# Second attention with global keys laid out on the diagonal, global values made in two parts, and the layernorm's scaling on ScalarE

## The reference

```python
Q, K, V = x @ Wq.T + bq, x @ Wk.T + bk, x @ Wv.T + bv   # 16 heads of 8
local = softmax(Q K^T / sqrt(8), over the keys at most 32 places away) @ V
Kg, Vg = K[:, global_indices], V[:, global_indices]     # 25 keys, the same for all
glob = softmax(Q Kg^T / sqrt(8)) @ Vg                   # a softmax of its own
out = (0.7 * local + 0.3 * glob) @ Wo.T + bo
```

## Time and profile before

| | us |
|---|---|
| median of 3 runs | 1109.08 (1107.51 to 1109.56) |
| profiled execution | 1103.31 |
| its span | 1101.6 |
| TensorE busy | 953.2 (87%) |
| VectorE busy | 781.5 (71%) |
| ScalarE busy | 577.6 (52%) |
| GpSimd busy | 678.9 (62%) |

### The profile page before, as it was taken

The page is one execution under the profiler, slowest core; times in us unless marked ns, Lnnn a source line. Parts: engine busy times, 40 slices in busy tenths (PEclk is TensorE's granted clock), DMA queues, the critical chain, the costliest instruction groups (busy, mean ns, idle before and its releaser), DMA issues.

```text
span 1101.6 us, 27734 instructions
## 1 busy us (share of the span) xinstructions
PE 953.2 (87%) x7536; PEld 699.0 (63%) x7536; DVE 781.5 (71%) x3615; ACT 577.6 (52%) x1250; POOL 678.9 (62%) x1491
## 2 busy tenths in 40 slices
PE   3999999999959995799999999999999319999940
PEld 1777777777735552677777777777776218777830
DVE  3788888888825776457786877777775327888846
ACT  2566676666621332255555555555545007777734
POOL 3566666666631322266769888887879523777765
PEclk9899999999978998599999999999989559999975
DMA  6121111211042441111112121212211166777717
GB/s 184 27 52 32 45 45 31 48 27 45 23 132 91 161 164 80 32 47 34 47 29 59 39 59 48 68 44 60 53 32 38 44 173 234 238 234 250 254 58 212
DMA packets 71375, 98.34 MB, mean 89 GB/s; under 512 B 13688, under 2 KB 43256, under 8 KB 71104
## 3 DMA queue, kind: packets, MB, share of 16 engines
q1 hardware_dynamic: 61040, 83.31, 25.9%
q0 software_dynamic: 4992, 10.30, 2.8%
q10 hardware_dynamic: 5232, 3.42, 1.2%
HBM read 49.48 MB, written 24.77 MB: 67 GB/s over the span
## 4 chain that ended last, share of the span: by engine, by line
PE 73%; DVE 10%; issue 5%; DMA 3%; POOL 3%; ACT 2%; SPq 2%; DVEq 0%; ACTq 0%; POOLq 0%
PE bank L342 6%; PE bank L172 5%; PE bank L253 5%; PE bank L351 4%; PE bank L372 4%; PE bank L1491 4%; PE bank L1492 4%; PE bank L1257 4%; PE bank L1493 4%; PE bank L406 4%; PE bank L168 3%; PE bank L413 3%; PE bank L346 3%; PE bank L381 3%; PE bank L398 2%
## 5 line engine op out<-in xcount | busy, mean ns | idle before, releaser
L528 ACT ACTIVATE p<-bank 128x480 f32<-128x480 f32 (+1 forms) x448 | 240.5, 540 | 247.8 <-PE bank L372 88.0
L663 DVE CUSTOM_DVE_ANT_0 bank<-bank,band 128x160 f32<-128x160 f32 x512 | 156.9, 347 | 82.0 <-PE bank L342 79.5
L663 DVE CUSTOM_DVE_ANT_0 bank<-bank,causal 128x128 f32<-128x128 f32 (+1 forms) x512 | 169.4, 386 | 56.1 <-PE bank L346 40.3
L893 POOL TENSOR_SCALAR_AFFINE_SELECT p<-p 128x380 f32<-128x380 f32 (+1 forms) x256 | 146.5, 602 | 57.2 <-ACT p L528 56.2
L1669 POOL DMA_INDIRECT y_rows<-p,rows x92 | 105.9, 1151 | 67.5 <-DVE p L1622 46.2
L663 DVE DVE_READ_ACCUMULATOR2_ANT nm<- 128x1 f32 x1024 | 143.6, 140 | 0.1
L874 POOL TENSOR_SCALAR_AFFINE_SELECT p<-p 128x256 f32<-128x256 f32 (+1 forms) x192 | 91.0, 486 | 68.3 <-ACT p L528 64.6
L342 PE MATMUL bank<-ks,qs 128*128 128x186 f32 x512 | 118.6, 316 | 3.5 <-issue 2.3
L342 PEld LDWEIGHTS bank<-ks,qs 128*128 128x128 f32 x512 | 81.5, 198 | 38.2 <-issue 23.3
L372 PE MATMUL bank<-qs,ks 128*128 128x160 f32 x512 | 102.2, 303 | 0.0
L1562 ACT ACTIVATE p<-bank,wb 128x512 f32<-128x512 f32 x92 | 63.6, 691 | 39.5 <-PE bank L1493 37.6
(11 more groups left out here) (207 smaller groups left out, 2330.0 us busy)
## 6 DMA issues: line engine op xcount, KB each, us to landing
qs<-parts SPq DMA_DIRECT2D x46, 512.0 KB, 5.2
qs<-qf SPq DMA_DIRECT2D x128, 128.0 KB, 2.4
rows<-xr SPq DMA_DIRECT2D x23, 260.0 KB, 3.7
parts<-ks SPq DMA_DIRECT2D x8, 512.0 KB, 2.8
xs<-x_b SPq DMA_DIRECT2D x16, 256.0 KB, 4.0
p<-in_w SPq DMA_DIRECT2D x12, 256.0 KB, 3.4
xin<-in_x SPq DMA_DIRECT2D x16, 128.0 KB, 2.2
parts<-qf SPq DMA_DIRECT2D x4, 512.0 KB, 2.7
```

The source lines that it names most:

```text
L528: act.activation(pb[:, :, :].rearrange("p u c -> p (u c)")[:, lo:lo + cols], bank[:, 0:cols], ACT.Exp, scale=SCALE).then_inc(L.exp_done, 1)
L663: return dve.tensor_tensor_reduce(at, at, mask, -1.0, -BIG, ALU.add, ALU.min, nm[:, item:item + 1])
L893: pool.affine_select(out=at, in_=at, compare_op=ALU.is_ge, fill=0.0, base=base, pattern=[[0, 4], [sign, hi - lo]], channel_multiplier=-sig ...
```

## The change

- **Global keys.** Unit 3 of pass 2 exists only for j = 2 and j = 3, for the sequence before. Each handles two t with one 128-column stationary part (`kg`, 25 keys of each of the four j on a block diagonal) and the unspread queries `qf`, 256 columns, in fp32r. `lay_out_kg` (VectorE, at (1, 2)) fills `kg` from the keys in `ks` and a mask. The rows of maxima are therefore sent twice, into the spread queries and into `qf`, which becomes a ring of three.
- **Global values.** `global_values(0)` at (3, 1) and `global_values(1)` at (0, 1) of the next iteration: four matmuls each, with the exponentials (`pg`) stationary and 64 columns of `vgb` moving. They give the sums already turned, in `T.og`; the copy of `og` and `round_og` are gone, and `normalise` reads `T.og`.
- **Banks.** `og` leaves the bank order; `rp` and `rt`, products of the routing, move to the end of (1, 1). `T.mi[1]` is free when its reader (the product with the local sums) is done.
- **Layernorm.** GpSimd also makes the shift, -mean times inverse deviation; ScalarE applies scale and shift at the end of the iteration, before `keep_pv` of the next.
- **Routing.** The last choice and the positions move to later places in VectorE's order, the sends by two or three j.

```diff
-ROUNDS = (("pj0", "og", "mx0", "ont", "mx1", "y", "q1", "xt", "mx3"),
-          ("rp", "ot", "pj1", "rt", "q0", "vg", "rl", "mx2", "k0", "k1", "kg"))
+ROUNDS = (("pj0", "mx0", "ont", "mx1", "y", "q1", "xt", "mx3"),
+          ("ot", "pj1", "rp", "rt", "q0", "vg", "rl", "mx2", "k0", "k1", "kg"))
...
+        def global_values(pair):
+
+            batch, par = (fin, p) if pair else (i - 1, n)
+            pe.wait_ge(L.exp_done, L.unit2(batch + 1, 2 + pair, 3) + 1)
+            if pair == 0:
+                pe.wait_ge(L.vg_kept, batch + 1)
+                wait(pe, L.on_done, batch)
             for tau in range(2):
+                out = T.og[:, tau * S:(tau + 1) * S].rearrange("p (r t z) -> p r t z", r=2, t=4)
+                for t in (2 * pair, 2 * pair + 1):
+                    m = pe.matmul(out[:, :, t, :], T.pg[pair][:, t % 2 * S + tau * P:t % 2 * S + (tau + 1) * P],
+                                  T.vgb[par][:, t, :].rearrange("p (r z) -> p r z", r=2),
+                                  start=tau == 0 and t == 0, stop=True, skip_group_check=True)
+            if pair:
+                m.then_inc(L.pg_done, 1)
...
             if L.local and u == 3:
-                for t in range(4):
-                    m = pe.matmul(bank[32 * t:32 * t + 32, 0:S], T.kg[par][:, t, :], q[:, t, :].bitcast(F32),
-                                  start=True, stop=True)
+                pe.wait_ge(L.kd_done, i)
+                for c in range(2):
+                    t = 2 * (j - 2) + c
+                    m = pe.matmul(bank[:, c * S:(c + 1) * S], T.kg[n][:, t, :], T.qf[(i - 1) % 3][:, t, :],
+                                  start=c == 0, stop=True, skip_group_check=True)
...
-            if part == 2:
-                if j == 0:
-                    pe.wait_ge(L.vg_kept, i)
-                pe.wait_ge(L.exp_done, 4 * step + 4)
-                m = pe.matmul(T.og[:, r * S:(r + 1) * S], T.vgb[n][:, j, :], pb[:, 3, 0:S],
-                              start=j == 0, stop=False, skip_group_check=True)
...
-                if j == 0 and u == 2 and th.finish and L.local:
-                    round_og()
...
+                if L.local and (j, u) == (3, 1) and th.late:
+                    global_values(0)
+                if L.local and (j, u) == (0, 1) and th.finish:
+                    global_values(1)
+                if (j, u) == (1, 1) and in_iteration("rp", i, p, th):
+                    round_rp()
+                if (j, u) == (1, 1) and in_iteration("rt", i, p, th):
+                    round_rt()
...
-            if L.local:
-                act.copy(T.ogs[:, :, :], T.og[:, :].rearrange("p (r q) -> p r q", r=2)).then_inc(L.ov_kept, 1)
...
+        def layernorm():
+            act.wait_ge(L.rstd, L.deviation_steps * (fin + 1))
+            for tau in range(2):
+                act.activation(W.x_next[:, 2 * fin + tau:2 * fin + tau + 1, :], T.r[:, tau:tau + 1, :], ACT.Identity,
+                               scale=T.rs2[:, tau:tau + 1], bias=T.shift[:, tau:tau + 1]).then_inc(L.x_out, 1)
...
+        if L.local and th.finish:
+            layernorm()
...
-            glob = T.mi[0][:, :].rearrange("p (h c) -> p h c", c=16)
+            glob = T.og[:, :].rearrange("p (h c) -> p h c", c=16)
...
+        def lay_out_kg():
+
+
+            wait(dve, L.p2_done, L.unit2(i - 1, 3, 3) + 1 if i > 1 else 0)
+            own = [P, 4, 4, NG]
+            keys = T.ks[p][:, :, 0:NG].bitcast(F32).rearrange("p t (o g) -> p t o g", o=1).to_broadcast(own)
+            mask = T.diag[:, ::DH].rearrange("p (a j o) -> p a j o", a=1, o=1).to_broadcast(own)
+            dve.tensor_tensor(T.kg[p].rearrange("p t (j g) -> p t j g", j=4)[:, :, :, 0:NG], keys, mask,
+                              ALU.mult).then_inc(L.kd_done, 1)
...
             pool.tensor_scalar(T.ve[:, :], T.mv[:, :, 1], EPS, None, ALU.add).then_inc(L.rstd, 1)
-            pool.wait_ge(L.rstd, 2 * fin + 1)
+            if L.local:
+                pool.tensor_scalar(T.shift[:, :], T.mv[:, :, 0], -1.0, None, ALU.mult).then_inc(L.rstd, 1)
+            pool.wait_ge(L.rstd, at + 1)
             pool.tensor_tensor(T.rs2[:, :], T.ve[:, :], T.mhalf[:, 0:2], ALU.pow).then_inc(L.rstd, 1)
+            if L.local:
+                pool.wait_ge(L.rstd, at + 3)
+                pool.tensor_tensor(T.shift[:, :], T.shift[:, :], T.rs2[:, :], ALU.mult).then_inc(L.rstd, 1)
...
             if p == 0 and i > 5:
-                send(i - 2, 3 + j, 4 + j)
-            elif p == 1 and j == 0 and i > 6:
-                send(i - 3, 7, 8)
-            elif i == B + 3 and j == 1:
+                send(i - 2, 1 + j, 2 + j)
+            elif p == 1 and j < 3 and i > 6:
+                send(i - 3, 5 + j, 6 + j)
+            elif i == B + 3 and j == 3:
                 send(i - 1, 0, 8)
-            elif p == 1 and j > 0 and i > 4 and i < B + 3:
-                send(i - 1, j - 1, j)
+            elif p == 1 and j == 3:
+                send(i - 1, 0, 1)
...
+                if L.local:
+                    qf = T.qf[(i - 1 if j == 0 else i) % 3]
+                    sp.dma_start(qf[32 * js + 24:32 * js + 24 + L.parts, :, :].bitcast(F32),
+                                 T.mt[js][0:4 * L.parts, :].bitcast(F32)).then_inc(L.mrow[js], 16)
```

More of the change, by code:

```diff
@@ L91, in __init__, with unit2 @@
             self.steps = 22
+    def unit2(self, i, j, u):
+        if not self.local:
+            return 3 * (4 * i + j - 3) + u
+        if i == 0:
+            return u
+        return 3 + 14 * (i - 1) + (0, 3, 6, 10)[j] + (u if j < 3 or i < B else u - 3)
 class There:
@@ L109, in max_step, with pass2_unit @@
         return self.late if j == 0 else self.scores
+    def pass2_unit(self, local, j, u):
+        if local and u == 3:
+            return self.late and j > 1
+        return self.pass2[j] and u < 3
 def iterations(eng, local, body):
@@ L174, in in_iteration @@
     def in_iteration(name, i, p, th):
-        if name in ("og", "vg", "kg", "rt", "rl", "rp") and not L.local:
+        if name in ("vg", "kg", "rt", "rl", "rp") and not L.local:
             return False
@@ L419, in pv @@
                                       start=False, stop=False, skip_group_check=True)
-            if part == L.kept:
+            if part == 1:
                 m.then_inc(L.pv_done, 1)
@@ L521, in exp @@
             pb = T.p[(j + 1) % 2]
-            bank = T.s2[u % 2 if L.local else (j + u) % 2]
-            cols = (S if u == 3 else len(local_items(u)) * WIN) if L.local else 512
-            act.wait_ge(L.p2_done, L.units * step + u + 1)
+            unit = L.unit2(i, j, u)
+            bank = T.s2[unit % 2 if L.local else (j + u) % 2]
+            act.wait_ge(L.p2_done, unit + 1)
+            if L.local and u == 3:
+                wait(act, L.pg_done, i - 1)
+                act.activation(T.pg[j - 2], bank[:, :], ACT.Exp, scale=SCALE).then_inc(L.exp_done, 1)
+                return
+            cols = len(local_items(u)) * WIN if L.local else 512
             if u == 0:
                 wait(act, L.pv_done, step - 1)
-            lo = 3 * WIN * u if L.local and u < 3 else 512 * u
+            lo = 3 * WIN * u if L.local else 512 * u
             act.activation(pb[:, :, :].rearrange("p u c -> p (u c)")[:, lo:lo + cols], bank[:, 0:cols], ACT.Exp,
@@ L608, in keep_vg @@
             dve.wait_ge(L.vg_done, i + 1)
-            wait(dve, L.pv_done, 4 * (i - 1))
-            vg = T.mi[1][:, 0:D].rearrange("p (t r s d) -> p r s t d", t=4, r=2, s=2)
-            out = T.vgb[p][:, :, :].rearrange("p (r s) (t z c) -> p r s t z c", r=2, t=4, z=2)
-            mask = T.diag[:, :].rearrange("p (t d) -> p t d", t=4)
-            for s in range(2):
-                for r in range(2):
-                    m = dve.tensor_tensor(out[:, r, s, :, s, 0:DH], vg[:, r, s, :, :], mask, ALU.mult)
-            m.then_inc(L.vg_kept, 1)
+            wait(dve, L.pg_done, i - 1)
+            vg = T.mi[1][:, 0:D].rearrange("p (t j d) -> p t j d", t=4, j=4)
+            out = T.vgb[p][:, :, :].rearrange("p t (j c) -> p t j c", j=4)
+            mask = T.diag[:, :].rearrange("p (o j d) -> p o j d", o=1, j=4).to_broadcast([P, 4, 4, DH])
+            dve.tensor_tensor(out[:, :, :, 0:DH], vg, mask, ALU.mult).then_inc(L.vg_kept, 1)
         def keep_kg():
```

148 lines of the change are left out of this document (75 added, 73 removed).

## The result

The changed kernel takes 1140.4 us (1135.7 to 1148.9) against 1108.3 (1101.2 to 1109.6) before: ratio 1.031, 95% interval 1.024 to 1.039. I had forecast 1099.8 and gave "slower" 0.2. The profiled execution took 1135.7 us, span 1133.9.

The account below looks back on a forecast made before the run. TensorE was taken to bound the kernel, new waits on VectorE and ScalarE meeting nearly all its gain; iterations, the stall with its low clock (-3.7) and tail (-1.1) total -9.3 us, giving 1099.8, range 1089 to 1115.

Parts of the forecast that it names:

- The other queues are covered: Second attention: SP's extra transfers come 6 us before use; GpSimd gets two 0.2 us instructions, idle 4.5 of 25 us.
- slower: the clock: Rival, 14%: new TensorE idles in each iteration lower its clock; 1128 us with a fall in every iteration.
- the idles of 0.6 and 1.15 us: Per iteration, TensorE waits 0.6 us for ScalarE's ov copy and 1.15 for VectorE in j=0, in two pieces.
- a wait that I have not seen, at 1112 or above: Rival, 6%: a wait not foreseen makes the kernel slower, 1112 us or above.
- The price of a fall: Each fall of TensorE's clock to half was taken to cost some 2.2 us.
- The tail: After 840 us: small instructions and ov wait +1.2 us, last x_b 2.3 us forward; -1.1 us in all.
- The stall at 814 us: TensorE's 1.48 us idle behind VectorE's slow layernorm goes, and 2.2 us of half clock after it; together -3.7.
- from pass 1 of (0,2) to that of (1,1): j=0 stretch: TensorE work falls from 4.64 to 2.8 us, VectorE still needs 3.9 plus 0.05 to release.
- The layout: VectorE's new diagonal layout of global keys, 0.66 us at its fastest, 1.3 at its slowest; taken as 1.0.
- ScalarE's queue at the turn: Key exponential, maxima row and two activations delay the ov copy to T+2.35; ov's transposes make TensorE wait 0.6 us.
- The even iteration: Even iterations 4 to 14: -2.18+1.15+0.6+0.1 = -0.33 us each; odd ones have 0.55 for 0.1, +0.12.
- TensorE's own gain: Per iteration, 4.58 us of work and wait leaves TensorE and 2.4 comes: 2.18 us gained.

Follow-up runs that it names:

- Experiment 1: Changed kernel with one line moved: GpSimd adds the bias (xb) after the masks of j=0, not ahead of those of j=2; 1118.1 us, ratio 1.009.
- 2: Changed kernel with the two matmuls of the new key unit at j=2 issued three times, same result; 1116.9 us, ratio 1.009.
- 5: Experiment 1 with ScalarE's two layernorm activations moved to just before its last exponential; 1113.9 us, ratio 1.014.
- 8: Experiment 1 with the second score unit of the last score iteration issued four times, ahead of the ov transposes; 1108.8 us, ratio 1.003.
- experiment 9: Changed kernel with five moves: xb early, layernorm earlier, normalise in two parts, router matmuls of j=1 later, maxima copied before the key exponential; 1105.4 us, ratio 0.998.
- experiment 12: Experiment 11 with the first-pass matmuls of j=0 and 1 issued twice in the last score iteration; 1083.1 us, ratio 0.982.
- experiment 11: Experiment 9 with router matmuls of j=1 right behind the transposes of on, ScalarE's copy and VectorE's positions fitted; 1085.6 us, ratio 0.983.
- The split: Changed kernel with VectorE's normalise in two parts: local values behind (0,2), global ones and sum behind (0,3); alone 1136.4 us, ratio 1.029.
- experiment 10: Kernel before with xb added between the two pairs of masks of j=2, 1.1 us later, nothing of the change; 1155.1 us, ratio 1.046.

## Why the prediction was wrong

**The step that failed** is "The other queues are covered", where I wrote off GpSimd because it idles 4.5 of 25 us. I had seen the residual wait for xb in the tail and did not ask the same of an iteration, where it already waited 0.52 us (634.70, above). GpSimd's idle time lies before the maxima of (0,3); from there to xb it has none. Three things of the change meet there: the maxima reach it 1.4 us later in even iterations and 0.3 in odd ones, TensorE wants the bank 0.5 us sooner, and the bank's reader stands behind both. In place of a covered queue the runs showed waits of TensorE of 0.9 to 1.2 us in most iterations from 6 on, 9.0 us in all, with falls of the clock behind most of them. Experiment 1 shows that this step is 22 us of the 32.

**The rival "slower: the clock"** was the right consequence and came by another wait. I had tied it to the idles of 0.6 and 1.15 us that I forecast. These came in pieces of 0.45, 0.23 and 0.6 and left the clock at 1.00 in iterations 2 to 5, and mostly in experiments 1 and 2. My 6% for "a wait that I have not seen, at 1112 or above" names what happened better than the 14% did. The rule of the Trainium skill that I cited ("TensorE: Matmul & The Clock Gate", section "A second HAM failure mode") has the direction right: short idles between groups on banks did let the clock swing. **The price of a fall was mis-sized**: I took 2.2 us for the one fall that I had, though its two windows, 816 to 824 us, at 0.63 and 0.52, come to an estimated 3.4 of 8 us. Some falls cost 1.7 (24.4 to 26.1), others 5 to 6 (24.6 to 29.7 and 31.0), because TensorE stays at 1.2 GHz for some 20 us and more. So 1128 for a fall in each iteration was too low.

**The tail:** I forecast -1.1 us and it took 7.9 more, in experiment 1 even 13.2. I had walked its waits, not its clock: its first 50 us had a mean clock of 0.67, in experiment 1 0.56, where before had 0.85 (the row in experiment 1). The stall at 814 us went as forecast, but not the low clock that I had counted with it: in experiment 1 the clock is at 0.83 in the window from 816 and at 0.50 from 820 to 860 us. That the clock explains the whole of the tail is not shown; the two runs meant to show it (5 and 8) lost it at the next wait.

**What was right**, by its size: values 0.91 us (534.11 to 535.02; I took 0.85); key unit 0.29 to 0.5 (0.35); from pass 1 of (0,2) to that of (1,1) 4.00 (3.95):

```profile
534.11 1.10 PE L251 MATMUL bank<-vgb,p 128*128 128x64 f32 x8
535.02 0.45 PE L366 MATMUL bank<-ks,qs 128*128 128x186 f32 x2
...
542.53 0.44 PE L366 MATMUL bank<-ks,qs 128*128 128x186 f32 x2
...
544.71 0.91 PE L275 MATMUL bank<-w_qkv,xt 128*128 128x384 f32 x2 [0.23 <-DVE on L630]
545.17 0.76 PE L398 MATMUL bank<-qs,ks 128*128 128x160 f32 x3
546.53 0.47 PE L366 MATMUL bank<-ks,qs 128*128 128x186 f32 x2 [0.61 <-DVE nm L710]
```

ScalarE's two activations took 0.87 us (0.82). The layout I had too dear: it took 0.57 us in most even iterations, 0.78 in the odd ones and 1.01 once (forecast 1.0). ScalarE's queue at the turn did hold TensorE, but at pj0, which waits for the maxima's row behind the exponential (0.45), and by then ov was there: I had the queue right and the first victim wrong. The even iteration at full clock came out at -0.32 (forecast -0.33), the odd one at +0.28 (+0.12), iterations 2 and 3 at -0.60 together (-0.8). The match in the even one is partly luck: the forecast waits are 1.29 us instead of 1.75, a wait of 0.37 before the product k0, behind ScalarE's row of maxima, was not in the sum, and TensorE's own gain, what is left, is 1.98 and not 2.18.

**Open:** what makes one wait drop the clock and another not. In the kernel after, windows with 3.17, 3.16 and 2.88 of 4 us busy kept it and windows with 3.12 and 3.16 lost it, and there and in experiment 9 waits of 1.02, 1.16 and 1.23 us stand on both sides. In experiment 12 three iterations have a short fall though the waits of the 6 us before it are only 0.20 and 0.38 us; these cost 1.2 us each (24.3 instead of 23.1). Its window:

```profile
572.00:576.00 4.00, 4.00 (x29) 3.74 (x27) 2.43 (x17) 2.20 (x6) 3.30 (x10) 0.57 0.03 10
```

So my theory that each fall starts with a wait of about a microsecond fits the long and dear falls, not the short ones, and such a wait does not always bring a fall. That the changed parts alone, without any wait of their own, would be faster than before is shown only together with the five moves; I did not give the kernel before moves of the same kind beyond xb. The split would, I expect, cost it a wait there (not tested), since the row of maxima uses the bank that its normalise reads.

## What to carry to other kernels

When you take work off a dense engine, list for each bank that it comes back to who reads it last and what that reader waits for, engine by engine: a queue with idle time elsewhere can have no slack at just this point. Price a new wait of about a microsecond in a TensorE-bound stream by the clock that it may cost (here from nothing to 6 us), not by its length alone, and look at the granted clock of each iteration first when a change disappoints. A change that loses may still be the better base: here five small moves in the order of work, one of them corrected in experiment 11, turned +3.1% into -1.7%.

## What was unexpected of the hardware

A fall can outlast its cause by far: after a wait of 1.23 us the clock stood at 0.50 in five windows of 4 us one after another, though TensorE was busy 4.00 of 4 us in four of them. 64 redundant instructions at the place of the wait made the kernel 23 us faster (ratio 1.009 against 1.031). And a VectorE instruction on 32 elements, usually 0.19 us, took 2.74 while GpSimd masked (experiment 10).
